# Pixel batches, a ring of rows and wide closing additions in a routed two-layer block (one core)

## The reference: what is computed

```python
def _L0_ffn_ref(x, Wr, br, W1, b1, W2, b2):
    xf = x.reshape(n, d)                      # n = 10368 tokens, d = 256
    logits = xf @ Wr.T + br                   # 8 experts
    probs = softmax(logits, axis=-1)
    top2_prob, top2_idx = jax.lax.top_k(probs, 2)
    comb = zeros((n, e)).at[arange(n)[:, None], top2_idx].add(top2_prob)
    h = gelu(einsum('nd,edh->enh', xf, W1) + b1[:, None, :], approximate=False)
    o = einsum('enh,ehd->end', h, W2) + b2[:, None, :]
    return einsum('ne,end->nd', comb, o)
...
x = x + _L0_conv_ref(_ln_c(x), ...)           # the mixer
t = _to_tokens(x)                             # (image, pixel, channel)
t = t + _L0_ffn_ref(_ln_t(t), ...)
x = _from_tokens(t, x)                        # (image, channel, pixel)
```

## Time and profile before

| what | value |
|---|---|
| median of three runs | 1770.32 us |
| profiled execution: time, span | 1765.54 us, 1763.8 us |
| busy: PE, DVE, ACT, POOL | 76%, 64%, 43%, 37% of the span |
| mean granted TensorE clock | 0.834 of full |
| DMA: bytes, packets | 250.50 MB, 310870 |
| routing (814.9 to 1068.4) | 253.5 us |
| experts (1068.4 to 1597.9) | 529.5 us |
| closing (1597.9 to 1763.8) | 165.9 us |

### The profile page before, as it was taken

One profiled execution on the slowest core, in us unless ns is written; L12 is line 12 of the kernel. 1 busy time (PEld: TensorE's weight loads), 2 busy tenths in 40 slices (PEclk: granted clock), 3 DMA queues, 4 the chain that ended last, 5 costly groups with the idle time before them and its releaser, 6 DMA issues.

```text
span 1763.8 us, 38992 instructions
## 1 busy us (share of the span) xinstructions
PE 1348.7 (76%) x9926; PEld 1129.9 (64%) x9927; DVE 1137.5 (64%) x3074; ACT 752.9 (43%) x1752; POOL 648.6 (37%) x561
## 2 busy tenths in 40 slices
PE   0393888979999999996565537999999999993222
PEld 0383888856767666666555535888888888882211
DVE  6894334327788888875888884666666666663333
ACT  0491444435454544444777743333333333331221
POOL 0260111113434343431666662545454454541000
PEclk9995878879999999995555558999999999995555
DMA  8534535467877887762443353323232323226999
GB/s 300 122 90 172 202 137 189 168 190 183 196 175 180 202 189 167 180 142 68 132 123 124 124 164 88 87 87 93 87 94 80 95 88 91 88 61 160 192 206 164
DMA packets 310870, 250.50 MB, mean 142 GB/s; under 512 B 184329, under 2 KB 289374, under 8 KB 310132
## 3 DMA queue, kind: packets, MB, share of 16 engines
q1 hardware_dynamic: 290527, 196.96, 43.2%
q0 software_dynamic: 20320, 53.28, 9.4%
HBM read 152.07 MB, written 105.57 MB: 146 GB/s over the span
## 4 chain that ended last, share of the span: by engine, by line
PE 53%; DVE 20%; DMA 11%; issue 7%; ACT 4%; SPq 3%; DVEq 1%; ACTq 0%; POOLq 0%; POOL 0%
PE ps L693 14%; PE ps L678 13%; DMA aux<-y_d 5%; PE ps L497 5%; PE ps L463 4%; ACT pool_ L1270 2%; PE ps L514 2%; PE ps L662 2%; DMA pool_<-k_d 2%; PE ps L479 2%; PE ps L541 2%; DVE pool_ L763 1%; PE ps L524 1%; DMA aux<-u_d 1%; PE ps L533 1%
## 5 line engine op out<-in xcount | busy, mean ns | idle before, releaser
L1494 POOL DMA_INDIRECT y_d<-pool_,to_s x176 | 254.7, 1447 | 285.6 <-DVE pool_ L1187 249.4
L693 PE MATMUL ps<-pool_,aux 128*128 x2112 | 248.7, 274 | 6.4 <-DVE aux L1179 3.5
L678 PE MATMUL ps<-aux,pool_ 128*128 128x256 f16 x2112 | 246.1, 273 | 1.0 <-ACT aux L1394 0.6
L693 PEld LDWEIGHTS ps<-pool_,aux 128*128 128x128 f16 x2112 | 199.4, 98 | 50.5 <-issue 25.6
L678 PEld LDWEIGHTS ps<-aux,pool_ 128*128 x2112 | 205.1, 98 | 26.6 <-issue 2.0
L1394 ACT ACTIVATE aux<-ps,b_s 128x256 f32<-128x256 f32 x352 | 138.0, 474 | 162.3 <-DVE aux L1179 161.9
L1474 POOL DMA_INDIRECT rows_d<-aux,idx_s x162 | 157.1, 970 | 101.8 <-DVE idx_s L1090 52.4
L1187 DVE SCALAR_TENSOR_TENSOR pool_<-ps,pool_ 128x512 f32<-128x512 f32 x88 | 60.8, 691 | 141.7 <-PE ps L693 141.7
L721 PE MATMUL ps<-ident_s,aux 128*128 128x128 f32 x162 | 41.7, 430 | 118.4 <-DVE aux L1219 118.4
L1466 POOL DMA_DIRECT2D pool_<-v_d x64 | 50.0, 781 | 216.4 <-PE ps L574 215.0
L1386 ACT ACTIVATE aux<-ps 128x512 f16<-128x512 f32 x88 | 52.5, 597 | 174.6 <-PE ps L662 174.6
(11 more groups left out here) (203 smaller groups left out, 3094.4 us busy)
## 6 DMA issues: line engine op xcount, KB each, us to landing
pool_<-rows_d SPq DMA_DIRECT2D x88, 258.0 KB
aux<-y_d SPq DMA_DIRECT2D x54, 384.0 KB, 6.7
big<-in_x SPq DMA_DIRECT2D x2, 5184.0 KB, 20.8
xn_d<-big SPq DMA_DIRECT2D x16, 648.0 KB, 3.0
v_d<-aux SPq DMA_DIRECT2D x64, 162.0 KB, 1.9
ks_d<-aux SPq DMA_DIRECT2D x64, 162.0 KB, 2.0
pool_<-xn_d SPq DMA_DIRECT2D x32, 324.0 KB
pool_<-k_d SPq DMA_DIRECT2D x32, 324.0 KB
```

Of the source, the lines that this page charges most:

```text
L678: last = nc.tensor.matmul(o, w_s[:, a, bass.ds(e * (4 * PIECE) + (k * HID + j * 128), 128)], xh_s[:, par, b, k * SLOTS:(k + 1) * SLOTS], s ...
L693: last = nc.tensor.matmul(ps[:, 6 + par, s * C:(s + 1) * C], hh_s[:, par, a, j, s * 128:(s + 1) * 128], w_s[:, b, bass.ds(e * (4 * PIECE) ...
L1494: nc.gpsimd.indirect_dma_start(out=y_d[:, :], out_offset=bass.IndirectOffsetOnAxis(ap=to_s[:, par, k:k + 1], axis=0), in_=yo_s[:, par, k, ...
```

## The change

Only routing, the tags, and closing change; the mixer and the matmuls of the experts stay.

- Routing goes over 8 batches of whole pixels (6, six times 12, then 3; a pixel is 128 tokens, one per image). PE reads the columns of a pixel straight from `x1_s`, 81 floats apart, for the logits and the transposes (`turn_pair`). ACT writes the transposed block back over the same places of `big` (`turned`), so that `big` ends with images on the partitions. DVE takes its statistics from there, and makes the choices for a whole batch at once (`choices`).
- ACT writes one normalised row and its four tags at a time into a ring of 18 rows (`rows`), and POOL sends each to its two places once it is there. From the second batch on, the rows of a batch stand behind the exponents of the next batch on ACT.
- A row's tags carry also its second weight and the difference to its first. In the expert stage DVE works out the weight of each row (two more small operations in `destinations`), and ACT multiplies the result by it (`weighed`, two more operations a tile) before POOL sends it.
- Closing is 9 chunks of 9 pixels: SP loads both results of a chunk (two DMAs in pieces of 9 KB, four chunks in flight), DVE adds both to `big` (two additions of 128 x 2304), and after the last SP stores `big` in two DMAs. ACT and PE have no part in it any more.
- Routing's loops are written out; the loops of the experts stay.

```diff
-SUBS = 3
-ROWS = SUBS * 128
-TURNS = BS * HW // ROWS
+BATCHES = (6,) + 6 * (12,) + (3,)
+FIRST = tuple(sum(BATCHES[:j]) for j in range(len(BATCHES) + 1))
+RING, BANKS = 18, 4
+CHUNK_P = 9
-WIDE = C + 2
+WIDE = C + 4
...
+        def pairs_of(j, part):
+            pairs = tuple(range(p, min(p + 2, FIRST[j + 1])) for p in range(FIRST[j], FIRST[j + 1], 2))
+            return pairs[0:1] if part == 0 else pairs[1:]
...
# SP, closing
+            for n in range(HW // CHUNK_P):
+                if n >= 4:
+                    sp.wait_ge(S["fin_d"], n - 3)
+                for k in range(2):
+                    rows = y_d[k * TOKENS:(k + 1) * TOKENS, :].rearrange("(b q) c -> b q c", q=HW)
+                    sp.dma_start(got_s[:, n % 4, k], rows[:, n * CHUNK_P:(n + 1) * CHUNK_P, :]
+                                 ).then_inc(S[f"gat{n % 4}"], 16)
+            sp.wait_ge(S["fin_d"], HW // CHUNK_P)
+            for h in range(HALVES):
+                sp.dma_start(out[:, h * half:(h + 1) * half], big[:, h * half:(h + 1) * half]).then_inc(S["out_s"], 16)
...
# PE, routing
+            def turn_pair(pair, j):
+                done = pair[0] // 2 - BANKS + 1
+                if done > 0:
+                    pe.wait_ge(S["turned_c"], done)
+                for p in pair:
+                    for h in range(HALVES):
+                        rows = x1_s[:, h, :].rearrange("c (b q) -> c q b", q=HW)[:, p, :]
+                        nc.tensor.matmul(ps[:, 4 + j % 2, at:at + EXPERTS], rows, router_s[:, h, :],
+                for k, p in enumerate(pair):
+                        last = nc.tensor.transpose(bank_of(pair)[:, k * C + h * 128:k * C + (h + 1) * 128],
+                                                   rows, ident_s[:, :])
...
+            for j in range(len(BATCHES)):
+                turn_pairs(j + 1, 0)
+                places(j)
+                turn_pairs(j + 1, 1)
...
# DVE, routing and closing
+            for j in range(len(BATCHES)):
+                pixel_parts(j + 1, 0)
+                positions(j)
+                low_piece(4 * j - 1)
+                pixel_parts(j + 1, 1)
+                low_piece(4 * j)
+                pixel_variance(j + 1)
+                low_piece(4 * j + 1)
+                choice_logits(j + 1)
+                low_piece(4 * j + 2)
+                choices(j + 1)
...
+            for n in range(HW // CHUNK_P):
+                sums = big[:, :].rearrange("b (c p) -> b c p", p=HW)[:, :, n * CHUNK_P:(n + 1) * CHUNK_P]
+                dve.wait_ge(S[f"gat{n % 4}"], 32 * (n // 4 + 1))
+                for k in range(2):
+                    ins = nc.vector.tensor_tensor(sums, sums, got_s[:, n % 4, k].rearrange("b q c -> b c q"), ALU.add)
...
# ACT, routing and experts
+            for j in range(len(BATCHES)):
+                turned(j + 1, 0)
+                if j == 0:
+                    rows(j)
+                turned(j + 1, 1)
+                high_piece(4 * j)
+                deviations(j + 1)
+                high_piece(4 * j + 1)
+                high_piece(4 * j + 2)
+                exponents(j + 1)
+                if j > 0:
+                    rows(j)
+                high_piece(4 * j + 3)
...
+            def weighed(t, par):
+                act.wait_ge(S["yo_c"], t + 1 + CREDIT)
+                for s in range(2):
+                    ins = nc.scalar.activation(yo_s[:, par, s, :], yo_s[:, par, s, :], ACT.Copy,
+                                               scale=wrow_s[:, par, s:s + 1])
+                ins.then_inc(S["yw_c"], 1)
...
# POOL, routing
+            for q in range(HW):
+                pool.wait_ge(S["xft_c"], q + 1)
+                for k in range(2):
+                    nc.gpsimd.indirect_dma_start(
+                        out=rows_d[:, :], out_offset=bass.IndirectOffsetOnAxis(ap=idx_s[:, k, q:q + 1], axis=0),
+                        in_=xf_s[:, q % RING, :], in_offset=None).then_inc(S[f"scat{q % RING}"], 16)
```

More of the change, by code:

```diff
@@ L25 @@
 CHUNK = 32
-AUX = 4640
+AUX = 8800
 TAP_ROWS = 64 + 11
@@ L359, in _ @@
             sp.wait_ge(S["pad_out"], 16 * (EXPERTS + 1))
-            for k in range(3):
-                sp.wait_ge(S[f"scat{k}"], 96 * (TURNS // 3))
+            for k in range(RING):
+                sp.wait_ge(S[f"scat{k}"], landed(HW - RING + (k - HW) % RING))
             sp.wait_ge(S["base_c"], 1)
@@ L635, in places, with turn_pairs @@
+            def turn_pairs(j, part):
+                if part == 0 and 2 <= j < len(BATCHES):
+                    pe.wait_ge(S["lgr_c"], j - 1)
+                for pair in pairs_of(j, part):
+                    turn_pair(pair, j)
+            def places(j):
+                pe.wait_ge(S["tot_c"], j + 1)
                 nc.tensor.matmul(ps[:, 7, 0:EXPERTS], before_s[:, :], tot_s[:, :], start=True, stop=True)
@@ L1368, in _, with exponents @@
-            tokens(0, 0)
-            tokens(1, 1)
-            deviations(0, 0)
-            rows(0, 0, 0)
-            with act.Fori(0, TURNS // 3 - 1) as i:
-                for k in range(3):
-                    act_turn(i * 3 + k, i, k)
-            for r in range(TURNS - 3, TURNS):
-                act_turn(r, r // 3, r % 3, ahead=TURNS - 1 - r)
-            for n in range(TURNS, PIECES):
-                high_piece(n, n % 3, n // 3 + 1)
+            def exponents(j):
+                if j >= len(BATCHES):
+                    return
+                n = BATCHES[j]
+                act.wait_ge(S["probs_c"], j + 1)
+                nc.scalar.activation(pr_s[:, 2, 0:n, :], pr_s[:, 1, 0:n, :], ACT.Exp).then_inc(S["ex2_c"], 1)
@@ new lines, in rows @@
+            def rows(j):
+                act.wait_ge(S["nmr_c"], j + 1)
+                act.wait_ge(S["idx_c"], j + 1)
+                for q in range(FIRST[j], FIRST[j + 1]):
+                    slot = q % RING
+                    act.wait_ge(S["turned_c"], q // 2 + 1)
+                    if q >= RING:
+                        act.wait_ge(S[f"scat{slot}"], landed(q - RING))
+                    nc.scalar.activation(xf_s[:, slot, 0:C], pixel_block(q), ACT.Identity,
+                                         bias=rs_s[:, q, 1:2], scale=rs_s[:, q, 0:1])
+                    nc.scalar.activation(xf_s[:, slot, C:WIDE], ptag_s[:, q, :], ACT.Copy).then_inc(S["xft_c"], 1)
@@ L1380, in _ @@
+            for n in range(4 * len(BATCHES), PIECES):
+                high_piece(n)
             act.wait_ge(S["tab_r"], 1)
```

488 lines of the change are left out of this document (188 added, 300 removed).

## The result

The changed kernel takes 1724.83 us (median of 4 runs, 1721.99 to 1730.86) against 1769.84 us for the kernel before on the same chip (4 runs): ratio 0.973, 95% interval 0.971 to 0.976, 45 us less. A second comparison on another chip gave 1727.10 against 1764.67 us, 0.980 (0.977 to 0.983), 38 us less. The prediction said 1754, 16 less, which is within 1% of before; its chances were 0.42 for faster by over 1% and 0.30 for within it. The time lies 0.8 us above the lower end of its eight-in-ten range (1724), and the forecast's own range (1738 to 1772) does not hold it.

A forecast was written before the change was run, and what follows sets the result against it. Routing was taken as bound by POOL and DVE, experts by PE, closing by the DMA engines; +29, +1.5 and -46 summed to -16 us, giving 1754 us. Forecast's own range 1738 to 1772, eight in ten 1724 to 1815.

The forecast's parts named there:

- POOL's wait: Routing: POOL idles 38 us between sixth and seventh pixel, because the second batch's rows stand behind the third's exponents on ACT.
- the covered weighing: Experts: ACT's two multiplications, some 0.95 us a tile, fall in its 1.83 us idle ahead of gelu; only the last tile uncovered.
- signs of being wrong: POOL idling in each batch, an expert tile growing from 5.75 us, or closing additions near 2.6 or 8.7 us.
- two rounds to the exponents of the third: Routing: each chain from one batch's exponents to the next's takes 31 us, so two take 2 x 31.
- 75 pixels on POOL: Routing: pixels after the first six cost POOL 2.63 us each, two scatters and 0.1 us of wait; scatters end at 276.7.
- 18 additions: Closing: DVE's additions of 2304 elements take 4.4 us each at the strided price, 79 us, covering the loads' 54.
- store with issue and end: Closing: 10.6 MB leave alone after the additions at 346 GB/s, 31 us, plus 1.5 for issue and end.
- The pair: Routing on PE: two pixels' logits and transposes from strided columns take 2.9 us, raised from 2.74 for contiguous pixels.
- the rival of strided PE: Routing: PE pays for strided columns, a pair takes 4.8 us, POOL starves in every batch; kernel 1815 us, chance 0.18.
- full-rate additions: Closing: rival in which DVE's additions take 2.6 us and loads set the pace; closing 93.5, kernel 1728 us, chance 0.20.
- additions that pay twice: Closing: rival in which each addition takes 8.7 us, 77 us more in all; kernel 1831 us, chance 0.10.
- a high clock in routing: Routing: rival in which PE gets 2.4 GHz, a pair takes 1.45 us, a round 24; kernel 1735 us, chance 0.07.

The follow-up runs named there:

- dense-column run: Changed kernel with PE's routing logits and transposes reading a contiguous 128 x 128 table instead of columns 324 bytes apart: routing 266.6 us, rounds of 27.8.

## Why the prediction was wrong

The mechanisms stood: the place and cause of POOL's wait, a POOL that is fed afterwards, the covered weighing, additions limited by DVE at the strided price, the store alone at the end. None of the prediction's signs of being wrong appeared. What failed are sizes, nearly all to the same side. By the prediction's own steps (us):

| step | forecast | measured |
|---|---|---|
| exponents of the first batch, after the start of routing | 16.5 | 13.8 |
| two rounds to the exponents of the third | 62 | 53.1 |
| first row and its scatter | 0.9 | 1.4 |
| 75 pixels on POOL | 197.3 | 194.4 |
| landing, checks, first tile | 5.75 | 5.6 |
| **routing** | **282.6** | **268.2** |
| experts against before | +1.5 | -0.8 |
| first chunk | 8 | 7.8 |
| 18 additions | 79 | 73.7 |
| store with issue and end | 32.5 | 26.4 |
| **closing** | **119.5** | **107.9** |

**The failed steps** are "*I raise the pair's eight passes to 1.85 ns a column and get 2.9 us*", where 2.50 were measured, "*the long store took 7.6 us ... 346 GB/s*", where the output left at 403, and "*2304 x 1.85 = 4.3 + 0.1 = 4.4*", where 4.12 were measured. Of the 28 us by which the sum was off, the store makes 6.1, the additions 5.3 and the thirteen pairs ahead of POOL's second batch some 5; the rest lies in the smaller steps.

- The pair. From the earlier trace rows I took 2.74 us for contiguous columns and raised it for a step that no row of PE showed to cost anything; five pairs of a round took 12.8 us for 14.5. The raise was 23 ns a pass, and the dense-column run shows 5. The 2.74 was too high itself, for a contiguous pair takes 2.45. In part this is because I had added the lengths of two groups that overlap: in the earlier trace rows the transposes end at 915.67 and the logits begin at 915.47. The Trainium skill ("SBUF — State Buffer", "Door 1: The DMA port swizzle") says that each access which crosses to a new 16-byte line pays. I had weighed that in the rival of strided PE; it fits DVE's additions (2.56 and 4.12 us) and not PE (347 and 352 ns).
- The rest of a round. 3.0 us for Ln and Exp came from a turn in which both table loads stood on the chain; with 12 variances to wait for, the first is hidden: 914.83 to 916.56, 1.7 us. And the first two rounds are shorter than a later one (26.0 and 27.1 us for 27.86); I priced both at 31. The first has the narrower operations of a batch of 6. In the second no rows of a batch stand ahead of the copies on ACT, which is the likely reason, but no run moved that alone.
- POOL's 0.1 us for the wait of each pixel was not there. The 75 pixels fell by only 2.9 us all the same, since the scatters took 993 ns on average and not 960.
- The store. A rate from one transfer of 2573.5 KB holds that transfer's own start and landing; I then added 1.5 us for issue and end again. The loads of the earlier trace rows gave 396 GB/s, and the output left at 403.
- The additions. Between 1.75 (L803, an addition like these) and 1.90 ns an element (L763, another operation) I took 1.85 and 0.1 us more; 4.12 us are 1.79. The price without a step was read from L908, which is a multiplication and not an addition; its 1.2 ns an element give 2.8 us, my 2.6 stands in no row, and 2.56 was measured.

Most were the careful choice between two values, and each careful choice made the kernel slower: 14.4 us in routing, 2.3 in the experts, 11.6 in the closing. The 2.3 of the experts are within the spread of that stage over the traces (526.6 to 531.1 us). Taken at the nearer row, the same sum changes so: a pair of 2.74 takes 2 us out of routing, no wait per pixel 7.5; 1.75 ns an element, with the 0.1 us kept, 4.6 out of the closing, 396 GB/s with nothing added 5.7. That is +19.5 + 1.5 - 56.3 = -35. One slip besides: the steps of routing add up to 282.4 and not 282.6, which changes nothing.

The rivals: full-rate additions exist (2.56 us), but only without the step, and would have given 84 us and not 93.5 of closing. That this rival's 1728 lies nearer to the measured time than the forecast is luck: its additions did not come, and the routing that it kept at +29 took half of that. Strided columns on PE, additions that pay twice and a high clock in routing (it stayed at 0.50) all fell.

## What to carry to other kernels

Take every unknown price at the row it is nearest to and put the careful end into the range; a sum of careful ends is no forecast, because their errors don't cancel. A rate for a long transfer is read from a long transfer, once, with its start in it. And on an engine that works in order, ask for each batch behind what it stands: rows moved ahead on ACT in all batches were worth 15 us, those of one batch alone nothing.

## What the runs showed of the hardware

- DVE's addition of 2304 fp32 elements: 1.11 ns an element with no stepping stream, 1.79 with one read at 1 KB, 1.85 with a read and the write at 324 bytes. A write that steps beside a read that does is nearly free. The Trainium skill ("VectorE: DVE Perf Modes", "Mode 1× (REGULAR) — the baseline") has one result a cycle, an estimated 1.04 ns at its 0.96 GHz: the first number fits, the others don't.
- 10.6 MB to DRAM: 26.4 us contiguous, 87.5 in pieces of 324 bytes. The Trainium skill ("DMA: Bandwidth & Descriptors", "Specifications") wants 512 bytes or more for the full rate and says that below this the DMA engine reads, modifies and writes. The pieces of 324 bytes agree with the limit, at a factor of 3.3; no run here shows the reading.
- POOL's scatter of expert rows takes 1447 ns on average if it starts right when DVE has added the biases, 987 if it starts some 0.9 us later, behind ACT. In the kernel before, such a scatter of 1.92 us (1154.94) starts 0.17 us into DVE's L1179 (1154.77 to 1156.00) and ends 0.86 us behind it; the changed kernel's of 0.98 us (1162.34) starts just after the same operation has ended (L1149, 1161.08 to 1162.31). That DVE's operation is the cause fits this, but no run moved it alone.
- The same mixer code took 810.6 to 824.2 us, at granted clocks of 0.80 to 0.82 between 170 and 300 us; its cause stays open.
